# A router's tail and a fill: moving small steps between the queues of a two-router transformer block on one core

## Chip, cores and metric

One NeuronCore of a Trainium2 chip runs the whole program in one launch. The metric is the device time of one execution in microseconds. Engines: TensorE (PE; its weight loads are PEld), VectorE (DVE), ScalarE (ACT), GpSimd (POOL), and SyncE (SP), which only issues DMAs. ScalarE and GpSimd issue DMAs too, from their own instruction streams.

## What is computed

The input x is 4096 rows (8 x 512 tokens) of 256 floats. Three layers, each added to x; the first and the last share their weights:

```python
x = x + 0.5 * ffn(layernorm(x))       # first router and experts ("a")
x = x + attn_block(layernorm(x))      # the middle
x = x + 0.5 * ffn(layernorm(x))       # second router and experts ("b")

# ffn: 8 experts, capacity 256 rows each (0.5 * 4096 / 8)
probs  = softmax(x @ w_switch + b_switch); routes = argmax(probs)
pos    = running count of the rows of the same route, up to this row, minus 1
keep   = pos < capacity
out    = where(keep, relu(x @ w1[e] + b1[e]) @ w2[e] + b2[e], x)
out    = out * (pmax / stop_gradient(pmax))

# attn_block: linear attention over the 16 heads of a token (feature map elu + 1),
# output projection, residual, layernorm, gelu MLP of width 1024, residual
```

A row that no expert keeps is "passed": its result is x + 0.5 * layernorm(x) times a factor near one, an affine function of the row. The kernel computes it for every row and stores it to the output; the experts later overwrite the rows that they keep.

## The kernel before

Rows are taken in 32 tiles of 128 (token tiles 0 to 31), in 8 groups of four. The order of the program is fixed by hand, one instruction stream per engine, with semaphores between them.

**Stages.** The first router and its experts come first, up to about 170 us. The middle is a software pipeline of 43 steps (MID_STEPS, s = 0 to 42): in step s, tile s is loaded and its statistics taken, tile s-2 is turned and multiplied to queries, keys and values, tiles s-3 to s-5 go through the attention, s-6 is normalized for the MLP. The MLP of group g takes steps 10 + 4g to 13 + 4g, two of its eight hidden blocks a step; its last products are in step 41 with the second down product in step 42. Then the second expert phase runs to the end: SyncE reads back the routing table (L453), VectorE makes token numbers, GpSimd gathers rows (L625), they are normalized and turned, and TensorE runs eight experts without a pause.

**Exchange of queries, keys and values (the fill).** Attention mixes heads within a token, so the three matrices are written to DRAM by SyncE (`store_grids`, L495) and read back in another layout by many small DMAs. A tile needs one DMA for values, eight for keys (`issue_keys`, L335) and eight for queries (`issue_queries`, L341). For the first HELPED = 7 tiles ScalarE issues six of the eight queries of a tile, and for tile 0 also four of its keys (L978 to L988). For tile 0 it does so in step 3, which in its program order stands ahead of `turn_zn(2)` (L902 to L906) in step 4, the copy of the turned tile 2 to `xnts[0]`, the high half of its operand; VectorE makes the low half (L1395) and TensorE then multiplies (`qkv`, in step 4 ahead of `sum_kv(0)`). `sum_kv(n)` (L1733) waits for the keys and values of tile n, `sum_att(n)` for its queries.

**Gelus.** In each step 10 to 41 ScalarE runs two hidden blocks (`gelus`, L933: once as float to `hid`, L941, once rounded to `hids`, L944); GpSimd subtracts the two (`low_hidden`, L726); TensorE multiplies by the down weights. The exponential and the gelu lie in different tables of ScalarE, so each change from one to the other is an ACT_TABLE_LOAD.

**Second router.** For group g: statistics on VectorE (`stats`, L1022), the inverse roots on GpSimd (`roots_b`, L586, whose two operations are L591 and L593), logits by TensorE, the choice on VectorE (`choose`, L1034), the exponential on ScalarE (`soften`, L790), the count of earlier rows on TensorE, and the dispatch on VectorE (`dispatch`, L1073), which leaves in `entry_b` and `dest_b` what is to be written where in the routing table. GpSimd then writes it with one indirect DMA per tile (`send`, L608 to L615, to `table`), computes four factors (`pass_factors_b`, L595), and VectorE makes the passed rows in `pass_b` (`passed`, L1097), a buffer of four tiles whose places come free when an earlier store has landed; SyncE stores them in pairs (`store_passed`, L402). Groups 0 to 5 are passed within the steps: `passed_at(s)` names the two tiles whose sends and rows fall in step s, tiles 20 and 21 in step 40, 22 and 23 in step 41. The router of group 6 runs in steps 40 to 42 (its `soften` in step 41 between the two gelu pairs), that of group 7 behind the steps, and tiles 24 to 31 are sent and passed there.

**What closes the middle.** SyncE reads the table only when all sends (`s_bsent`), all passed rows' stores (`s_bstored`) and all stores of the residual rows x2 to `late_rows` (`s_x2s`) have landed; the other engines wait for the same semaphores.

Of the kernel before, what the change touches and what calls it, by code (L numbers as in the profile page):

```python
# [14 lines left out]
P = 128  # L15
# [12 lines left out]
def build(nc, x_in, ln1_w, ln1_b, wq, bq, wk, bk, wv, bv, wo, bo, ln2_w, ln2_b,  # L28
# [32 lines left out]
    with ExitStack() as ctx:  # L61
# [84 lines left out]
        s_bsent, s_bstored = sems("b_sent", 2), sems("b_stored", 2)  # L146
        one = {f: sem(f"experts_{f}") for f in ("table", "token", "stat", "root", "unit", "turned", "xt", "xtl",
# [180 lines left out]


# [60 lines left out]
        def _(sp):  # L390
# [11 lines left out]
            def store_passed(n):  # L402

                sp.wait_ge(s_bmade, n + 2)
                sp.dma_start(out_rows[n * P:(n + 2) * P, :].rearrange("(t p) d -> p t d", p=P),
                             pass_b[:, n % GROUP:n % GROUP + 2]).then_inc(s_bstored[n // 2 % 2], 16)

# [140 lines left out]
            for n in range(PASSED_IN_STEPS, NT, 2):  # L548
                store_passed(n)
# [3 lines left out]
            sp.wait_ge(s_bmade, NT)  # L553
# [13 lines left out]
        def _(pool):  # L567
# [166 lines left out]
            for s in range(MID_STEPS):  # L734
# [5 lines left out]
                for n in passed_at(s):  # L740
                    send(n)
# [11 lines left out]
                if group_at(s, 16) is not None:  # L753
                    roots_b(group_at(s, 16))
                if routed(s, 2) is not None:
                    pass_factors_b(routed(s, 2))


            roots_b(NG - 1)
            for n in range(PASSED_IN_STEPS, (NG - 1) * GROUP):  # L760
                send(n)
            pass_factors_b(NG - 1)
            for n in range((NG - 1) * GROUP, NT):
# [13 lines left out]
        def _(act):  # L777
# [148 lines left out]

            def copy_kvt(n):
# [22 lines left out]
            for s in range(MID_STEPS):  # L950
                if at(s, 2) is not None:
                    turn_zn(s - 2)
                g_up, j_up = divmod(s - 10, GROUP)
# [22 lines left out]
                if routed(s, 1) is not None:  # L976
                    soften(routed(s, 1))
                n = at(s, 3)  # L978
                if n is not None and n < HELPED:
                    act.wait_ge(s_grid[n % 2], 16 * (n // 2 + 1))  # L980
                    if n == 0:
                        act.wait_ge(s_zeros, 6)
                        for t in range(4, 8):
                            issue_keys(act, 0, t)
                    if n >= 2:
                        act.wait_ge(s_st2, n - 1)
                    for t in range(2, 8):
                        issue_queries(act, n, t)  # L988
# [12 lines left out]

            g = NG - 1
# [4 lines left out]
            identify(g)  # L1007

# [3 lines left out]
            act.wait_ge(s_bmade, NT)  # L1012
# [8 lines left out]
        def _(dve):  # L1021
# [51 lines left out]
            def dispatch(g):  # L1073
# [14 lines left out]
                if g >= 2:  # L1088
# [6 lines left out]
                                         op0=ALU.mult, op1=ALU.mult).then_inc(s_bdisp, 1)  # L1095

# [414 lines left out]
            for n in range(PASSED_IN_STEPS, NT):  # L1511
                passed(n)
# [435 lines left out]
```

## Time and profile before

| | |
|---|---|
| median of 3 runs | 772.32 us (770.03 to 772.68) |
| the profiled execution | 771.66 us |
| its span in the trace | 769.9 us |
| busy in the span | PE 87%, PEld 75%, DVE 58%, ACT 52%, POOL 42% |
| mean granted clock of TensorE | 0.94 of full |

All rows are of the one profiled execution, in microseconds from its span's start. The difference between its time and its span, 1.8 us, lies around the trace. A row of the timeline has the start, the length, the engine and line, the operation with its output and inputs, the count of merged instructions, and in brackets how long the engine stood idle before it and what ended that. A line number can be that of a small helper (L1527 is every matmul, L1539 every transpose), so tile names say which one it is. "q" behind an engine is its instruction queue, where DMA issues are.

### The profile page before, as it was taken

What the parts mean: (1) busy time and instruction counts of PE and PEld (TensorE: products, weight loads), DVE (VectorE), ACT (ScalarE), POOL (GpSimd) and SP (SyncE); (2) the same over time, 40 slices, a digit from 0 to 9 for tenths busy, and PEclk for the clock granted to TensorE, in tenths of its full rate; (3) what the DMA queues carried; (4) which work ended last, traced back from release to release, by engine and by line L of the source; (5) the groups of instructions that cost most, each with busy time, mean ns of one, the idle gap of its engine ahead of it and who ended that gap; (6) DMA issues with size and microseconds to landing.
All of it is one profiled execution on the core that took longest, in us unless ns stands there. A gap on an engine that the chain in (4) does not pass through costs nothing. (4 is left out here: it accounts for less than half of the span.)

```text
span 769.9 us, 17017 instructions
## 1 busy us (share of the span) xinstructions
PE 671.6 (87%) x6127; PEld 578.8 (75%) x6127; DVE 447.3 (58%) x1222; ACT 400.8 (52%) x805; POOL 326.5 (42%) x480
## 2 busy tenths in 40 slices
PE   7649999984777999999999999999999822999993
PEld 5437999973555888888888888888888712999993
DVE  7852756413477676767868677777565352444420
ACT  5753555512333667676766767666736510444430
POOL 6240573322132343444554745636456664133311
PEclk9759999996899999999999999999999975999997
DMA  8485677413665454544655455545415232466610
GB/s 261 141 277 174 199 253 237 135 38 75 100 110 92 80 83 84 93 82 65 108 79 126 66 110 91 97 78 95 81 42 169 91 117 42 132 205 198 209 59 28
DMA packets 284001, 92.43 MB, mean 120 GB/s; under 512 B 213933, under 2 KB 281636, under 8 KB 283918
## 3 DMA queue, kind: packets, MB, share of 16 engines
q1 hardware_dynamic: 267310, 82.26, 44.9%
q0 software_dynamic: 4096, 8.33, 3.4%
q10 hardware_dynamic: 12512, 0.76, 1.1%
q8 instruction: 50, 0.82, 0.4%
q14 instruction: 33, 0.27, 0.1%
HBM read 61.95 MB, written 29.41 MB: 119 GB/s over the span
## 5 line engine op out<-in xcount | busy, mean ns | idle before, releaser
L1527 PE MATMUL bank<-down_w,hids 128*128 128x256 f32 x768 | 107.9, 285 | 1.9 <-POOL hids L726 1.9
L726 POOL TENSOR_TENSOR hids<-hid,hids 128x512 fp32r<-128x512 f32 x64 | 83.1, 1298 | 54.2 <-ACT hids L944 54.0
L1527 PE MATMUL bank<-hnts,up_w 128*128 128x512 f32 x384 | 104.4, 407 | 0.0
L1527 PEld LDWEIGHTS bank<-down_w,hids 128*128 128x128 f32 x768 | 97.3, 188 | 5.5 <-POOL hids L726 3.5
L1527 PE MATMUL bank<-qkv_w,xnts 128*128 128x256 f32 (+1 forms) x384 | 80.9, 361 | 12.6 <-DVE xnts L1395 11.8
L1527 PEld LDWEIGHTS bank<-qkv_w,xnts 128*128 128x128 f32 x384 | 64.0, 199 | 25.6 <-DVE xnts L1395 14.0
L1527 PEld LDWEIGHTS bank<-hnts,up_w 128*128 128x128 f32 x384 | 67.6, 189 | 11.4
L941 ACT ACTIVATE hid<-bank,cols 128x512 f32<-128x512 f32 x64 | 44.1, 688 | 45.7 <-PE bank L1527 45.4
L717 POOL TENSOR_SCALAR sth<-sth 128x1 f32<-128x1 f32 x32 | 7.2, 225 | 129.9 <-DVE sth L1407 129.8
L1527 PE MATMUL bank<-b_w,xb_h 128*128 128x256 f32 x256 | 60.1, 379 | 0.0
L1527 PE MATMUL bank<-a_w,xa_h 128*128 128x256 f32 x256 | 60.1, 379 | 0.0
L1527 PE MATMUL bank<-xb_xt,b_w 128*128 128x256 f32 x384 | 58.0, 304 | 1.5 <-DVE xb_xt L1136 1.5
L1527 PE MATMUL bank<-xa_xt,a_w 128*128 128x256 f32 x384 | 58.1, 304 | 1.4 <-DVE xa_xt L1136 1.4
L825 ACT ACTIVATE xb_h<-bank,cols 128x256 f32<-128x256 f32 x64 | 26.9, 471 | 60.1 <-PE bank L1527 50.1
L1527 PEld LDWEIGHTS bank<-xa_xt,a_w 128*128 128x128 f32 x384 | 51.9, 199 | 3.7 <-DVE xa_xt L1136 1.8
L1527 PEld LDWEIGHTS bank<-xb_xt,b_w 128*128 128x128 f32 x384 | 51.9, 199 | 3.4 <-DVE xb_xt L1136 1.9
L825 ACT ACTIVATE xa_h<-bank,cols 128x256 f32<-128x256 f32 x64 | 26.8, 470 | 51.6 <-PE bank L1527 48.5
L1527 PEld LDWEIGHTS bank<-b_w,xb_h 128*128 128x128 f32 x256 | 46.3, 189 | 5.1
L1527 PEld LDWEIGHTS bank<-a_w,xa_h 128*128 128x128 f32 x256 | 46.3, 189 | 5.1
L906 ACT CAST xnts<-bank 128x256 fp32r<-128x256 f32 x32 | 12.0, 375 | 63.1 <-PE bank L1539 58.0
L1110 DVE TENSOR_TENSOR b_w<-b_raw,b_w 128x512 fp32r<-128x512 f32 x32 | 24.0, 751 | 35.8 <-ACT b_w L806 18.0
L944 ACT ACTIVATE hids<-bank,cols 128x512 fp32r<-128x512 f32 x64 | 43.6, 681 | 0.0
(246 smaller groups left out, 1426.2 us busy)
## 6 DMA issues: line engine op xcount, KB each, us to landing
qkv_rows<-feats SPq DMA_DIRECT2D x32, 384.0 KB, 3.5
a_raw<-in_L_ffn_w_dram SPq DMA_DIRECT2D x32, 256.0 KB
a_w<-in_L_ffn_w_dram SPq DMA_DIRECT2D x32, 256.0 KB
b_raw<-in_L_ffn_w_dram SPq DMA_DIRECT2D x32, 256.0 KB
b_w<-in_L_ffn_w_dram SPq DMA_DIRECT2D x32, 256.0 KB
mid_rows<-x_all SPq DMA_DIRECT2D x8, 512.0 KB
x<-mid_rows SPq DMA_DIRECT2D x32, 128.0 KB, 2.6
values<-qkv_rows SPq DMA_DIRECT2D x32, 128.0 KB
```

The costliest lines, as they stand in the source:

```text
L717: pool.tensor_scalar(st[:, 7:8], st[:, 7:8], EPS, None, ALU.add).then_inc(rs, 1)
L726: pool.tensor_tensor(hids[1][u % 3][:], hid[u % 2][:], f32(hids[0][u % 3][:]), ALU.subtract).then_inc(s_hidl, 1)
L825: act.activation(ex.buf.h[u % 4][:, i], dst[:, i * CAP:(i + 1) * CAP], ACT.Relu, bias=bias).then_inc(ex.sem.relu, 1)
L906: act.copy(xnts[0][n % 2][:], bank[B_TURN][:, 0:D].rearrange("p (k t) -> p k t", k=KD)).then_inc(s_xnh, 1)
L941: act.activation(hid[u % 2][:], bank[b][:], ACT.Gelu, bias=bias).then_inc(s_hid, 1)
L944: act.activation(hids[0][u % 3][:], bank[b][:], ACT.Gelu, bias=bias).then_inc(s_hid, 1)
L1110: dve.tensor_tensor(low[cut], ex.raw[cut], f32(high[cut]), ALU.subtract).then_inc(ex.sem.low1, 1)
L1527: return pe.matmul(dst, left, right, start=start, stop=stop, skip_group_check=True)
```

## The change

Three things move.

1. Fill: ScalarE's six query issues for tile 0 go from step 3 to step 4, behind `turn_zn(2)`. Its four key issues stay in step 3.
2. Second router, group 6: the exponential goes behind the gelus of step 41, the roots ahead of step 40's second subtraction, the count on TensorE behind the down product of step 41. GpSimd sends one tile in step 40 (20) and one in step 41 (21) instead of two; 22 to 25 follow behind the steps ahead of the roots of group 7, then 26 to 31.
3. Passed rows of groups 6 and 7: the factors are computed on VectorE behind the last dispatch, the rows of tiles 24 to 27 by ScalarE and of 28 to 31 by VectorE, and they overwrite their place in `x2` instead of going to `pass_b`. SyncE stores them from there.

```diff
@@ sync @@
+            def store_in_place(n):
+                g, first = n // GROUP, n % (2 * GROUP)
+                sp.wait_ge(s_bplace[g % 2], n % GROUP + 2)
+                sp.dma_start(out_rows[n * P:(n + 2) * P, :].rearrange("(t p) d -> p t d", p=P),
+                             x2[:, first:first + 2]).then_inc(s_bstored[n // 2 % 2], 16)
             for n in range(PASSED_IN_STEPS, NT, 2):
-                store_passed(n)
+                store_in_place(n)
...
-            sp.wait_ge(s_bmade, NT)
+            sp.wait_ge(s_bmade, PASSED_IN_STEPS)
@@ gpsimd, LAST_SENT = PASSED_IN_STEPS - GROUP @@
-                for n in passed_at(s):
-                    send(n)
+                if group_at(s, 16) == NG - 2:
+                    roots_b(NG - 2)
+                if s < MID_STEPS - 3:
+                    for n in passed_at(s):
+                        send(n)
+                if s == MID_STEPS - 2:
+                    send(LAST_SENT + 1)
...
                     low_hidden(g_up, 2 * j_up + 1)
-                if group_at(s, 16) is not None:
+                if s == MID_STEPS - 3:
+                    send(LAST_SENT)
+                if group_at(s, 16) is not None and group_at(s, 16) < NG - 2:
                     roots_b(group_at(s, 16))
-                if routed(s, 2) is not None:
+                if routed(s, 2) is not None and routed(s, 2) < NG - 2:
                     pass_factors_b(routed(s, 2))
+            for n in range(LAST_SENT + 2, PASSED_IN_STEPS + 2):
+                send(n)
             roots_b(NG - 1)
-            for n in range(PASSED_IN_STEPS, (NG - 1) * GROUP):
-                send(n)
-            pass_factors_b(NG - 1)
-            for n in range((NG - 1) * GROUP, NT):
+            for n in range(PASSED_IN_STEPS + 2, NT):
                 send(n)
@@ scalar @@
+            def help_queries(n):
+                act.wait_ge(s_grid[n % 2], 16 * (n // 2 + 1))
+                if n >= 2:
+                    act.wait_ge(s_st2, n - 1)
+                for t in range(2, 8):
+                    issue_queries(act, n, t)
             for s in range(MID_STEPS):
                 if at(s, 2) is not None:
                     turn_zn(s - 2)
+                if s == 4:
+                    help_queries(0)
...
-                if routed(s, 1) is not None:
+                if routed(s, 1) is not None and routed(s, 1) < NG - 2:
                     soften(routed(s, 1))
...
+                if s == 3:
+                    act.wait_ge(s_grid[0], 16)
+                    act.wait_ge(s_zeros, 6)
+                    for t in range(4, 8):
+                        issue_keys(act, 0, t)
+                if at(s, 3) is not None and 1 <= s - 3 < HELPED:
+                    help_queries(s - 3)
...
+            soften(NG - 2)
             g = NG - 1
...
             soften(g)
             identify(g)
+            for n in range(PASSED_IN_STEPS, (NG - 1) * GROUP):
+                g, i = divmod(n, GROUP)
+                act.wait_ge(s_bfac, 4 * (g + 1))
+                act.wait_ge(s_x2s[g % 2], 16 * (g // 2 + 1))
+                row = x2[:, n % (2 * GROUP)]
+                act.activation(row, row, ACT.Identity, bias=fac_b[g % 2][:, 2, i:i + 1],
+                               scale=fac_b[g % 2][:, 3, i:i + 1]).then_inc(s_bplace[g % 2], 1)
@@ vector: pass_factors_b as on GpSimd before, and @@
+            def passed_in_place(n):
+                g, i = divmod(n, GROUP)
+                dve.wait_ge(s_bfac, 4 * (g + 1))
+                dve.wait_ge(s_bturn, n + 1)
+                dve.wait_ge(s_x2s[g % 2], 16 * (g // 2 + 1))
+                row = x2[:, n % (2 * GROUP)]
+                dve.tensor_scalar(row, row, fac_b[g % 2][:, 3, i:i + 1], fac_b[g % 2][:, 2, i:i + 1], ALU.mult,
+                                  ALU.add).then_inc(s_bplace[g % 2], 1)
             dispatch(g)
-            for n in range(PASSED_IN_STEPS, NT):
-                passed(n)
+            pass_factors_b(NG - 2)
+            pass_factors_b(NG - 1)
+            for n in range((NG - 1) * GROUP, NT):
+                passed_in_place(n)
@@ tensor @@
                 g = routed(s, 1)
-                if g is not None:
+                if g is not None and g < NG - 2:
                     pe.wait_ge(*kv_free)
                     count(g, bank[B_KV])
...
                     down_mid(g_up, 2 * j_up)
+                if g == NG - 2:
+                    pe.wait_ge(*kv_free)
+                    count(g, bank[B_KV])
+                    kv_free = (s_bdisp, 9 * g + 1)
```

## Rows read from the trace of the kernel before

**Rows 1.** Chain that ended last, in order of time: start, length, what.
```profile
634.13 2.13 DMA table<-rb_entry,rb_dest
636.31 2.74 DMA xb_table<-table
...
650.14 6.99 PE bank L1527 x36
```

**Rows 2.** Timeline, steps 41 and 42.
```profile
611.31 1.55 PE L1527 MATMUL bank<-hnts,up_w 128*128 128x512 f32 x6
...
611.60 0.19 DVE L1039 TENSOR_TENSOR rb_lg<-bank,rb_rstd 128x32 f32<-128x32 f32 x1 [1.32 <-POOL rb_rstd L593]
...
613.55 1.28 ACT L941 ACT_TABLE_LOAD   x1
...
614.84 0.69 ACT L941 ACTIVATE hid<-bank,cols 128x512 f32<-128x512 f32 x1
...
616.00 0.62 ACT L806 CAST b_w<-b_raw 128x512 fp32r<-128x512 f32 x1
616.19 1.26 POOL L726 TENSOR_TENSOR hids<-hid,hids 128x512 fp32r<-128x512 f32 x1 [0.76 <-ACT hids L944]
...
617.50 1.71 PE L1527 MATMUL bank<-down_w,hids 128*128 128x256 f32 x12 [1.62 <-POOL hids L726]
617.92 0.18 DVE L1071 TENSOR_TENSOR rb_cnt<-bank,rb_hot 128x32 f32<-128x32 f32 x1
...
619.25 1.42 DVE L1419 TENSOR_TENSOR x_<-bank,xr 128x256 f32<-128x256 f32 x4
```

**Rows 3.** Timeline, behind the steps, to the last send.
```profile
622.34 0.23 POOL L591 TENSOR_SCALAR rb_rstd<-rb_mv 128x4 f32<-128x4 f32 x1 [2.40 <-DVE rb_mv L1032]
...
623.80 0.19 DVE L1039 TENSOR_TENSOR rb_lg<-bank,rb_rstd 128x32 f32<-128x32 f32 x1 [1.54 <-POOL rb_rstd L593]
...
626.54 0.20 DVE L1094 SCALAR_TENSOR_TENSOR rb_entry<-rb_small 128x4 f32<-128x4 f32 x1
...
629.94 1.46 DVE L1103 TENSOR_SCALAR rb_pass<-x_,rb_fac 128x256 f32<-128x256 f32 x4 [1.66 <-DMA out_dram<-rb_pass]
630.16 1.10 POOL L613 DMA_INDIRECT table<-rb_entry,rb_dest  x1 [0.34 <-issue]
...
634.13 0.97 POOL L613 DMA_INDIRECT table<-rb_entry,rb_dest  x1 [0.30 <-issue]
```

**Rows 4.** Timeline, fill, ScalarE's queue, ScalarE and TensorE.
```profile
189.49 3.17 ACTq L341 DMA_DIRECT2D queries<-qkv_rows  x6
...
193.03 0.37 ACT L906 CAST xnts<-bank 128x256 fp32r<-128x256 f32 x1 [5.11 <-issue]
...
193.92 4.21 PE L1527 MATMUL bank<-qkv_w,xnts 128*128 128x512 f32 x12 [5.97 <-DVE xnts L1395]
```

**Rows 5.** Timeline of SyncE's queue, keys of tiles 1 and 6.
```profile
194.69 4.50 SPq L335 DMA_DIRECT2D keys<-qkv_rows  x8
...
241.44 5.86 SPq L335 DMA_DIRECT2D keys<-qkv_rows  x8
```

**Rows 6.** Waits of SyncE's queue, 186 to 300: total, times, longest.
```profile
SPq L505 <- DMA qkv_rows<-feats: 14.9, 8, 3.5
...
SPq L495 <- DVE feats L1465: 1.0, 3, 0.4
```

**Rows 7.** Timeline of TensorE's weight loads, `sum_kv(6)`.
```profile
250.18 0.81 PEld L1527 LDWEIGHTS bank<-keys,values 128*32 128x32 f32 x32 [0.52 <-DMA keys<-qkv_rows]
```

**Rows 8.** Line L863: ns min/median/max; tile rb_pass from 626 to 632: landing.
```profile
L863 ACT ACTIVATE x_all<-x_all,ra_small x32: 583/586/604, 27.6 to 46.0; 128x256 f32<-128x256 f32 x32
...
DMA to landing us min/median/max: 2.2/2.2/2.2
```

**Rows 9.** Windows, 629.5 to 630: busy per engine, clock, DMA share, GB/s.
```profile
629.50:630.00 0.50, 0.00 (x0) 0.00 (x0) 0.06 (x1) 0.00 (x0) 0.33 (x2) 0.50 1.01 340
```

**Rows 10.** Windows, 650 to 658, same columns.
```profile
652.00:654.00 2.00, 2.00 (x12) 2.00 (x11) 0.74 (x2) 0.89 (x3) 0.10 (x1) 0.50 0.00 0
654.00:656.00 2.00, 2.00 (x12) 2.00 (x12) 0.69 (x1) 0.79 (x2) 0.00 (x0) 0.56 0.00 0
656.00:658.00 2.00, 2.00 (x18) 1.97 (x18) 0.69 (x1) 1.85 (x6) 0.00 (x0) 1.00 0.41 131
```

More of the change, by code:

```diff
@@ L146, in build @@
         s_bsent, s_bstored = sems("b_sent", 2), sems("b_stored", 2)
+        s_bplace = sems("b_passed_in_place", 2)
         one = {f: sem(f"experts_{f}") for f in ("table", "token", "stat", "root", "unit", "turned", "xt", "xtl",
@@ L327, in build @@
         PASSED_IN_STEPS = (NG - 2) * GROUP
+        LAST_SENT = PASSED_IN_STEPS - GROUP
         HELPED = 7
@@ L975, in _ @@
                     copy_kvt(0)
-                if routed(s, 1) is not None:
+                if routed(s, 1) is not None and routed(s, 1) < NG - 2:
                     soften(routed(s, 1))
[L978 to L988, printed above, removed]
+                if s == 3:
[5 more added lines that the diff above has]
+                    help_queries(s - 3)
                 for n in turned_at(s, 0):
@@ L1007, in _ @@
             identify(g)
+            for n in range(PASSED_IN_STEPS, (NG - 1) * GROUP):
[5 more added lines that the diff above has]
+                               scale=fac_b[g % 2][:, 3, i:i + 1]).then_inc(s_bplace[g % 2], 1)
             for i in range(2):
                 act.wait_ge(s_bsent[i], 64 * (NG // 2))
-            act.wait_ge(s_bmade, NT)
+            act.wait_ge(s_bmade, PASSED_IN_STEPS)
             for i in range(2):
@@ L1095, in dispatch, with pass_factors_b @@
                                          op0=ALU.mult, op1=ALU.mult).then_inc(s_bdisp, 1)
+            def pass_factors_b(g):
+                w, wm, shift, factor = (fac_b[g % 2][:, i] for i in range(4))
+                dve.wait_ge(s_bdisp, 9 * (g + 1))
+                dve.wait_ge(s_bfac, 4 * g)
+                dve.tensor_tensor(w, entry_b[g % 2][:, :, 1], rstd_b[g % 2][:], ALU.mult).then_inc(s_bfac, 1)
+                dve.wait_ge(s_bfac, 4 * g + 1)
+                dve.tensor_tensor(wm, w, mv_b[g % 2][:, :, 0], ALU.mult).then_inc(s_bfac, 1)
+                dve.tensor_scalar(factor, w, 1.0, None, ALU.add).then_inc(s_bfac, 1)
+                dve.wait_ge(s_bfac, 4 * g + 2)
+                dve.tensor_scalar(shift, wm, -1.0, None, ALU.mult).then_inc(s_bfac, 1)
+            def passed_in_place(n):
[6 more added lines that the diff above has]
+                                  ALU.add).then_inc(s_bplace[g % 2], 1)
             def passed(n):
```

## The prediction

> **What bounds the kernel now.** I read the chain that ended last first. Behind the middle of the kernel it is one straight line: the last send of routing entries lands at 634.13 + 2.13 = 636.26 us, the table is read back at 636.31, rows are gathered and normalized, and from 650.14 on TensorE multiplies to the end [rows 1]. So every microsecond by which the table read comes earlier is a microsecond of the span, if nothing behind it changes, and nothing behind it is edited. The timeline then shows what holds the table read. In step 41, the last with up-projections, ScalarE swaps to its exponential table and back for one small activation: TensorE's product is ready at 611.31 + 1.55 = 612.86, the load back ends at 614.83 and the gelu starts at 614.84 [rows 2]. The exponential was late because VectorE's choice waited 1.32 us for the inverse roots of GpSimd, which stood behind two sends and a subtraction [rows 2]. TensorE stood 1.62 us before its last down product at 617.50 [rows 2]. After that comes the router of the last group, entries at 626.74, and then GpSimd alone: sends of 0.97 us with 0.30 us between them, 1.28 us from start to start, the last at 634.13 [rows 3]. In the fill I read ScalarE's queue beside TensorE: six query issues take 3.17 us from 189.49, the high half of token tile 2 (the third xnts) follows at 193.03, and TensorE has stood 5.97 us when its product starts at 193.92 [rows 4].
>
> **Fill: the six issues go behind the third high half.** Nothing is added or removed: ScalarE starts the cast at about 189.5 instead of 193.03, 3.5 us earlier, and TensorE its product at 190.4. SyncE's queue is passed by none of this, and that is why I take zero. From 194.69 SyncE sends rows, stores and eight key loads per tile back to back: eight keys cost between 4.50 and 5.86 us [rows 5]. Of its waits between 186 and 300 us, 14.9 us are for the landing of its own stores and only 1.0 for VectorE's features [rows 6], so compute hardly paces it. The keys of tile 6, issued from 241.44 to 247.30, are what TensorE's weight load at 250.18 waits for (0.52 us, ended by the keys) [rows 5, 7]. A TensorE that runs 3.5 us ahead at 190 meets the same keys by then. Bounds: 3.5 us of gain if the keys were no limit, and a loss if ScalarE's issues for tile 1, now some 3.5 us earlier and so inside SyncE's window from 194.69, slow SyncE: at most 5.86 - 4.50 = 1.36 us for a tile [rows 5]. I take 0, nearest to the row at 250.18.
>
> **Steps 40 and 41.** GpSimd takes the roots of group 6 ahead of the second subtraction and only one send a step instead of two. The roots move ahead of that subtraction, so VectorE's choice, at 611.60 before, loses its wait of 1.32 us for them [rows 2]. ScalarE runs the last gelu right behind TensorE's product: 612.9 instead of 614.84, 1.9 us earlier. GpSimd's subtraction followed the gelu by 616.19 - 614.84 = 1.35 us, TensorE the subtraction by 1.31 us [rows 2]: 614.3 and 615.6. The single send between two subtractions (1.28 us after 612.6) ends at 613.8 and fits. TensorE fills 612.9 to 614.9 with the count and the other down product, which cost 0.4 and 1.7 us. The exponential itself pays a table load of 1.28 us behind the gelus (over at 614.2) and the weight cast of 0.62 us [rows 2]: it is over at 616.3. From the reading of the counts to the residual sum VectorE took 619.25 - 617.92 = 1.33 us [rows 2]; a first part of that lies before the exponential, so dispatch and count update are over at 617.5. The residual sum, 619.25 before, needs TensorE (615.6 + 1.7 = 617.3) and VectorE (617.5) [rows 2]. **Term: 1.75 us gained.** Both engines arrive within 0.2 us of each other, so nothing is to spare. Group 7's exponential then finds its table loaded; its load before was hidden behind the roots, so that counts nothing.
>
> A weighing of a rule: the row shows the load at 613.55 lasting 1.28 us and the gelu 0.01 us behind it, so a swap costs 1.28 us here [rows 2]. The Trainium skill (ScalarE: Activation LUTs, What ACT_TABLE_LOAD costs) adds a drain of 1.38 us to every switch, 2.66 in all. By that the exponential behind the gelus would be over 1.4 us later and the sum would be 3.1 us of gain instead of 4.5; this trace disagrees with the drain.
>
> **GpSimd behind step 41.** Four sends (22 to 25) start at 615.7 and end with 4 x 1.28 at 620.8. The statistics of group 7 were ready for the roots at 622.34 [rows 3]; 1.75 earlier is 620.6. So the roots start at 620.9, **0.3 us given back**, 1.45 gained. Roots to choice took 623.80 - 622.34 = 1.46, choice to entry 626.74 - 623.80 = 2.94 [rows 3]: choice at 622.35, entries at 625.3. Sends 26 and 27 lie between (622.5 to 625.0) and hide; before, all four sends of group 6 and the pass factors stood there and held send 28 until 630.16, 3.4 us behind the entries [rows 3]. Now send 28 starts at 625.4 and send 31 at 625.4 + 3 x 1.28 = 629.25 against 634.13: **4.9 us gained**, the 1.45 in it. The landing took 2.13 us with an empty queue [rows 1]. Now it shares the queues with the last stores of passed rows; its bounds are 0 and another 1 us (a store takes 2.2 us from issue to landing, and a send that meets one could see up to half of it [rows 8]). I take 0.4 us: last landing 631.8, **table read 4.5 us earlier**.
>
> **Factors and rows in place.** VectorE gets eight small operations behind the entries; by the spacing of the small ones in the router, about 0.12 us each, factors of group 6 at 625.8 and 7 at 626.3. Two places make the rows: ScalarE four of group 6, costed by the rows of the first stage, 0.586 us each [rows 8], done by 628.2; VectorE four of group 7, 1.46 us for four [rows 3], done by 627.8. Neither waits for a buffer; before, four rows waited 1.66 us for a store [rows 3]. What they wait for instead is that the store of x2 has landed, and that one is issued right behind the residual sum, over 6 us before. SyncE issues four stores at 627.0, 627.8, 628.3 and 628.8; landing 2.2 us later [rows 8] is 631.0. By volume, 1 MB at 340 GB/s [rows 9] is 3.1 us from about 628.2: 631.3. So this path lies 0.1 to 0.5 us below the sends: hidden, with a thin cover. If it were 1 us late, it would set the table read and cost 0.5 us. The final wait of SyncE and ScalarE on passed rows is shortened to 24 tiles and costs nothing.
>
> **Sum.** 0 (fill) - 4.5 (end of the middle) = -4.5 us against the profiled execution: 771.66 (span 769.9, 1.8 around it) becomes 767.2. The median of the runs is 772.32, 0.66 above that execution, so 767.8. Bounds of the main case: 5.0 gained with a landing of 2.13, 3.5 with a landing 1.4 us longer. TensorE's granted clock adds a scatter that no edit sets: after the long wait it stood at half level (1.2 GHz) and rose between 654 and 656, some 5 us after the products began at 650.14 [rows 1, 10]. A rise two microseconds sooner or later would move the end by one, since half the rate does half the work; the three runs spread over 2.65 us.
>
> **The rivals.**
> (a) The fill pays: the keys would come in time after all. For it: TensorE's 5.97 us stand is real [rows 4], and the first product there also starts closer to the one before, so it may find the higher clock. Against: the wait for keys at 250.18 [rows 7]. With 2.5 of the 3.5 us kept, 765.3.
> (b) The end gives only part: the sends' landing, the rows in place on ScalarE, or the exponential take the place of the removed waits. Place: the table read. If the passed rows or the exponential chain come 2 us later than worked out, the gain is 2.5 and the time 769.8. For it: three chains meet within 0.5 us of each other. In its own sentence, one form of it: VectorE's rows in place while GpSimd makes descriptors. The rows show sends of 0.97 us alone and 1.10 beside VectorE's rows at 629.94 [rows 3], 0.1 us; if instead the four rows (1.46 us) held the sends up wholly, the gain would be 3.0 and the time 769.3, 3 in 100. The Trainium skill (SBUF — State Buffer, SBUF: two separate sides) has that rule: GpSimd cannot write descriptors while VectorE holds the shared port with such an operation. The rows here bear out a tenth of it.
> (c) Slower: ScalarE's query issues fall into SyncE's key issues and slow them. Place: the fill, keys of tiles 1 to 7. Price: 1.36 us a tile [rows 5], 7 x 1.36 = 9.5 us, less 4.5: 5.0 slower, 777.3. It turns the sign from the fourth tile on (4.5 / 1.36 = 3.3). Against: only the first one or two tiles are shifted, since TensorE's lead is gone at the next keys.
> (d) The edits do not reach the chain, because another wait (store of x2, storing of passed rows) holds the table read: 772.3.
>
> **How the numbers follow.** Main case 0.62, (a) 0.08, (b) 0.22, (c) 0.05, (d) 0.03. A measurement of this kernel can tell about 0.5%, 3.9 us. The main case at 4.5 with half a microsecond of doubt passes that in nine tenths: 0.56 + 0.08 from (a) = 0.64 faster; (c) gives 0.05 slower; the rest, 0.31, is within. The range reaches from 765.5 (5.0 gained, and the scatter of the clock, or (a)) to 770.3 (case (b)), and leaves out (c), (d) and the far end of (a).
>
> **What would show it.** Right: in the fill TensorE's product of tile 2 starts near 190.4, yet the keys' product of tile 6 stays near 250.2, with a wait ended by keys. The last gelu 0.1 us behind its product; no table load between the gelus of step 41; residual sum near 617.5; roots of group 7 right behind send 25 at 620.9; last send near 629.3; no stand of VectorE before its last rows; table read near 631.8. Wrong: a table read held by the stores of passed rows, keys earlier or later than 250 by over 1 us, or roots of group 7 after 622.

## The result, and the profile after

The changed kernel takes 765.15 us (median of 5 runs, 763.97 to 766.51), the kernel before 770.29 us in the same rounds (median of 5, 769.61 to 772.68). The ratio is 0.9925, interval 0.9902 to 0.9949: 5.1 us faster by the medians, 5.8 by the ratio. A second series of the change has 0.9935 (0.9922 to 0.9948), 5.0 us. The forecast was 767.8 us with a range of 765.5 to 770.3: the way was right and the gain of 4.5 us close to what was measured, but the time lies 0.35 us under the range. The kernel before was no longer at 772.32: with two more runs its median is 770.29, and four later series of it have 769.51 to 770.90.

The profiled execution of the changed kernel took 766.51 us, span 764.8. First the end of the middle, in the order of the prediction. The timeline of the changed kernel around steps 41 and 42 (lines are of the changed program: L1578 is every matmul, L735 GpSimd's subtraction, L622 its send):

```profile
605.45 1.05 POOL L602 TENSOR_TENSOR rb_rstd<-rb_rstd,minus_half 128x4 f32<-128x4 f32 x1
...
609.11 0.18 DVE L1067 TENSOR_TENSOR rb_lg<-bank,rb_rstd 128x32 f32<-128x32 f32 x1
...
610.22 1.56 PE L1578 MATMUL bank<-hnts,up_w 128*128 128x512 f32 x6
610.29 1.28 POOL L735 TENSOR_TENSOR hids<-hid,hids 128x512 fp32r<-128x512 f32 x1 [0.17 <-ACT hids L966]
...
610.44 1.18 DVE L1082 TENSOR_TENSOR rb_hot<-first_wins,rb_best 128x32 bf16<-128x32 f32 x1
...
611.82 0.69 ACT L963 ACTIVATE hid<-bank,cols 128x512 f32<-128x512 f32 x1 [1.53 <-PE bank L1578]
...
613.61 1.28 ACT L809 ACT_TABLE_LOAD   x1
...
614.48 1.69 PE L1578 MATMUL bank<-down_w,hids 128*128 128x256 f32 x12 [1.03 <-POOL hids L735]
...
616.49 1.42 DVE L1468 TENSOR_TENSOR x_<-bank,xr 128x256 f32<-128x256 f32 x4
```

Against [rows 2]: the roots are done at 606.50, so VectorE's choice at 609.11 has no wait for them; the last gelu starts at 611.82, 0.04 us behind the product that ends at 611.78; the table load stands behind the gelus at 613.61. TensorE still stands ahead of its last down product, but 1.03 us instead of 1.62. The residual sum follows the first gelu of step 41 (608.93) by 7.56 us; before, that gelu started at 609.80 and the distance was 619.25 - 609.80 = 9.45. Behind the steps:

```profile
618.69 0.97 POOL L622 DMA_INDIRECT table<-rb_entry,rb_dest  x1 [0.30 <-issue]
...
619.69 0.24 POOL L600 TENSOR_SCALAR rb_rstd<-rb_mv 128x4 f32<-128x4 f32 x1
...
621.16 0.19 DVE L1067 TENSOR_TENSOR rb_lg<-bank,rb_rstd 128x32 f32<-128x32 f32 x1 [1.66 <-POOL rb_rstd L602]
...
623.88 0.16 DVE L1122 SCALAR_TENSOR_TENSOR rb_entry<-rb_small 128x4 f32<-128x4 f32 x1
...
624.56 2.08 ACT L1034 ACTIVATE x_<-x_,rb_fac 128x256 f32<-128x256 f32 x4 [2.18 <-DVE rb_fac L1135]
...
624.88 0.98 POOL L622 DMA_INDIRECT table<-rb_entry,rb_dest  x1 [1.27 <-DVE rb_entry L1122]
...
625.23 1.38 DVE L1143 TENSOR_SCALAR x_<-x_,rb_fac 128x256 f32<-128x256 f32 x4
625.68 2.41 SPq L414 DMA_DIRECT2D out_dram<-x_  x4
626.16 0.97 POOL L622 DMA_INDIRECT table<-rb_entry,rb_dest  x1 [0.31 <-issue]
...
628.72 0.97 POOL L622 DMA_INDIRECT table<-rb_entry,rb_dest  x1 [0.30 <-issue]
630.99 0.37 SPq L462 DMA_DIRECT2D xb_table<-table  x1
```

Against [rows 3]: the roots of group 7 start 0.03 us behind send 25, which is the send at 618.69; VectorE and ScalarE make their rows with no wait for a buffer; the last send is at 628.72 and the table is read at 630.99, 22.06 us behind the first gelu of step 41 instead of 26.51. That is 4.45 us, against 4.5 forecast for this part. What SyncE waited for last, by its own waits in the stretch (total, times, longest), is the stores first and then, for 0.3 us, the sends:

```profile
SPq L564 <- DMA out_dram<-x_: 2.4, 1, 2.4
SPq L566 <- DMA table<-rb_entry,rb_dest: 0.3, 1, 0.3
```

The fill is the second half. The same stretch as [rows 4], and on to the keys of tiles 1 and 3:

```profile
187.33 0.37 ACT L921 CAST xnts<-bank 128x256 fp32r<-128x256 f32 x1 [2.42 <-issue]
187.36 3.03 ACTq L344 DMA_DIRECT2D queries<-qkv_rows  x6
...
188.22 4.21 PE L1578 MATMUL bank<-qkv_w,xnts 128*128 128x512 f32 x12 [3.94 <-DVE xnts L1444]
...
199.98 1.82 PE L1578 MATMUL bank<-keys,values 128*32 128x128 f32 x32 [2.50 <-DMA keys<-qkv_rows]
...
202.08 3.04 PE L1578 MATMUL bank<-qkv_w,xnts 128*128 128x512 f32 x12
...
219.78 1.17 PE L1578 MATMUL bank<-keys,values 128*32 128x128 f32 x32 [1.60 <-DMA keys<-qkv_rows]
...
221.22 3.66 PE L1578 MATMUL bank<-qkv_w,xnts 128*128 128x512 f32 x12
```

The cast now stands ahead of the six issues, and TensorE's product of tile 2 starts after a stand of 3.94 us instead of 5.97. But TensorE then stands 2.50 us for the keys of tile 1 and 1.60 us for those of tile 3, where it had stood 0.56 us and less before. And its clock falls behind these stands: the product of tile 3 at 202.08 took 3.04 us and that of tile 5 at 221.22 took 3.66 us, where others take 2.37.

### The profile page after: what moved, and what is told of

The parts are those of the page before. It is cut to its first block, busy times and chain, and to the rows that moved or that the text cites. A ratio compares the mean times of both kernels' runs of the same rounds, so it can differ in the third digit from the quotient of the medians.

```text
span 764.8 us, 17021 instructions
## 1 busy us (share of the span) xinstructions
PE 672.3 (88%) x6127; PEld 580.9 (76%) x6127; DVE 446.1 (58%) x1226; ACT 400.6 (52%) x807; POOL 325.4 (43%) x472
## 4 chain that ended last, share of the span: by engine, by line
PE 56%; issue 5%; DMA 4%; POOL 3%; DVE 3%; ACT 3%; SPq 2%; ACTq 1%; POOLq 0%; DVEq 0%
PE bank L1578 51%; PE bank L1590 5%; DMA qkv_rows<-feats 2%; SPq L338 2%; POOL hids L735 1%; ACTq L344 1%; POOL table L622 1%; DMA keys<-qkv_rows 1%; DMA xb_rows<-late_rows,xb_token 0%; ACT hids L966 0%; ACT feats L936 0%; DMA xb_table<-table 0%; ACT ots L989 0%; DMA mid_rows<-xa_fin,xa_slot 0%; DMA table<-rb_entry,rb_dest 0%
## 5 line engine op out<-in xcount | busy, mean ns | idle before, releaser
L1578 PE MATMUL bank<-down_w,hids 128*128 128x256 f32 x768 | 107.8, 285 | 1.3 <-POOL hids L735 1.3
L735 POOL TENSOR_TENSOR hids<-hid,hids 128x512 fp32r<-128x512 f32 x64 | 83.1, 1299 | 54.7 <-ACT hids L966 54.5
L1578 PE MATMUL bank<-hnts,up_w 128*128 128x512 f32 x384 | 104.5, 407 | 0.0
L1578 PEld LDWEIGHTS bank<-down_w,hids 128*128 128x128 f32 x768 | 97.3, 188 | 4.9 <-POOL hids L735 2.9
L1578 PE MATMUL bank<-qkv_w,xnts 128*128 128x256 f32 (+1 forms) x384 | 81.9, 364 | 9.2 <-DVE xnts L1444 8.4
L1578 PEld LDWEIGHTS bank<-qkv_w,xnts 128*128 128x128 f32 x384 | 64.9, 202 | 21.9 <-DVE xnts L1444 10.0
L1578 PEld LDWEIGHTS bank<-hnts,up_w 128*128 128x128 f32 x384 | 67.6, 189 | 11.4
L1578 PE MATMUL bank<-b_w,xb_h 128*128 128x256 f32 x256 | 60.1, 379 | 0.0
L1578 PE MATMUL bank<-a_w,xa_h 128*128 128x256 f32 x256 | 60.1, 379 | 0.0
L1578 PE MATMUL bank<-xb_xt,b_w 128*128 128x256 f32 x384 | 58.2, 304 | 1.5 <-DVE xb_xt L1185 1.5
L1578 PE MATMUL bank<-xa_xt,a_w 128*128 128x256 f32 x384 | 57.7, 303 | 1.4 <-DVE xa_xt L1185 1.4
L1578 PEld LDWEIGHTS bank<-xb_xt,b_w 128*128 128x128 f32 x384 | 52.0, 199 | 3.4 <-DVE xb_xt L1185 1.9
L1578 PEld LDWEIGHTS bank<-xa_xt,a_w 128*128 128x128 f32 x384 | 51.6, 198 | 3.7 <-DVE xa_xt L1185 1.8
L1578 PEld LDWEIGHTS bank<-b_w,xb_h 128*128 128x128 f32 x256 | 46.3, 189 | 5.1
L1578 PEld LDWEIGHTS bank<-a_w,xa_h 128*128 128x128 f32 x256 | 46.3, 189 | 5.1
L1514 DVE SCALAR_TENSOR_TENSOR feats<-bank,feats 128x512 f32<-128x512 f32 x32 | 22.1, 691 | 37.9 <-ACT feats L938 37.9
```

Source lines behind the costliest of these rows:

```text
L735: pool.tensor_tensor(hids[1][u % 3][:], hid[u % 2][:], f32(hids[0][u % 3][:]), ALU.subtract).then_inc(s_hidl, 1)
L1514: dve.scalar_tensor_tensor(out=soft, in0=bank[B_QK][:], scalar=0.0, in1=soft, op0=ALU.max, op1=ALU.add).then_inc(s_feat, 1)
L1578: return pe.matmul(dst, left, right, start=start, stop=stop, skip_group_check=True)
```

## Experiments

All of them are built on one of the two kernels; "ratio" is to the kernel before in the same rounds. Since the edits are local, each profile is also cut at fixed events, in us: A, the first load of a row of the middle (all before it is untouched everywhere); B, from SyncE's first key load of tile 0 to the first gelu of step 41 (the fill and the steps); C, from there to the table read; D, from the first product of the second expert phase to the end of the span (untouched everywhere). Between A and B lie another 16.1 to 17.2 us that no edit touches, and between C and D 13.7 to 14.0.

| kernel | A | B | C | D |
|---|---|---|---|---|
| before, shown ahead | 171.37 | 422.33 | 26.51 | 119.76 |
| before again | 169.26 | 422.80 | 26.55 | 119.97 |
| change | 169.08 | 423.43 | 22.06 | 119.94 |
| change again | 169.63 | 421.69 | 22.32 | 119.03 |
| fill only | 169.25 | 423.91 | 27.18 | 118.99 |
| fill only again | 169.38 | 421.72 | 26.59 | 118.58 |
| end only | 169.41 | 422.15 | 22.06 | 118.84 |
| change, fill delayed | 169.74 | 420.40 | 22.06 | 119.72 |
| the same again | 169.56 | 420.93 | 22.08 | 119.45 |
| change, store first | 169.87 | 421.29 | 22.66 | 118.97 |
| change, delay and store first | 169.37 | 423.02 | 22.02 | 118.65 |
| change, rows not in place | 168.70 | 422.98 | 24.03 | 118.58 |
| change, exponential between | 168.69 | 424.39 | 24.32 | 119.93 |
| change, sends paired | 169.97 | 421.68 | 23.87 | 119.59 |

### Halves of the change

Fill only, on the kernel before:

```diff
+                if s == 4:
+                    help_queries(0)
...
-                if n is not None and n < HELPED:
+                if at(s, 3) is not None and 1 <= s - 3 < HELPED:
```

> Only the fill edit, on the kernel before. Theory A (SyncE's queue paces the fill): TensorE's product of tile 2 starts about 3.5 us sooner behind the keys of tile 0, but sum_kv of tile 6 comes within 1 us of where it was behind the keys of tile 0 (62.7 us behind, 250.18 - 187.47), and the time stays within 1 us of before: ratio 0.9990 to 1.0010. Rival B (the fill pays): up to 3.5 us less, ratio down to 0.9955, sum_kv(6) 2.5 us or more sooner. Rival C (ScalarE's earlier issues or stores landing behind queries slow SyncE): 1 to 4 us more, ratio 1.0013 to 1.005.

769.19 us (median of 11) against 769.51, ratio 0.9984 (0.9969 to 1.0): 0.3 us less by the medians and 1.2 by the ratio, while its profile has B at 423.91, over 1 us longer than before. So a second time:

> The fill edit alone, again, for a second profile and more rounds. Theory A: within 1.2 us of before (ratio 0.9985 to 1.0015); TensorE stands 2 us or more ahead of the keys' product of tile 1 and its clock falls there. Rival B (the fill edit is worth the 1 us that the first rounds hinted at, 0.9984 with an interval of 0.9969 to 1.0): ratio 0.9985 or less again.

769.09 us (median of 12) against 770.77, ratio 0.9978 (0.9966 to 0.999), and B at 421.72. By the two ratios the fill edit is worth 1.2 and 1.7 us, against my zero, and B lies 2 us apart in two profiles of one program. The kernel before against itself shows how far such a ratio strays:

> The kernel before as it is, against itself: ratio 0.999 to 1.001, which shows how far such a ratio strays. Theory A (the first profile of before was a slow draw in the untouched first stage, 171.4 us to the first row load where eleven profiles of other kernels have 168.7 to 170.0): 168.7 to 170.0 now, profiled time 769 to 770.5. Rival B (before has a slower first stage than every edited kernel): 171 again. Keys of tile 0 to first gelu of step 41 near 422.2, no half-clock stretch behind 208 us in either case.

770.85 against 770.9, ratio 0.9993 (0.9978 to 1.0008), A at 169.26, B at 422.80. So the first profile of the kernel before had a long A by 2 us. The time of this one, 771.34, lies above what was expected all the same: its span is 768.6, and 2.7 us lie around it instead of 1.8. The fill edit's 1.2 and 1.7 us stand against a stray of 0.5 us; only the second series excludes zero.

End only, which is the change without the lines above:

> The change without its fill edit. Theory A: the whole gain is here, ratio 0.993 to 0.9945 (4.3 to 5.3 us less); from the first gelu of step 41 to the table read 22.1 us, as in the changed kernel (630.99 - 608.93), against 26.5 before (636.31 - 609.80). Rival B: 2.5 us of the gain is the fill's, ratio 0.9965 or more. Rival C: more gain than the change has, ratio under 0.992.

765.31 us (median of 7) against 769.51, ratio 0.995 (0.9932 to 0.9967), C at 22.06. The ratio lies just over the 0.9945 that was expected, with an interval that holds it. The stretch C gives 4.45 us on the trace and the time gave 3.9 us by the ratio: the end carries the bulk of the gain, and 1 us or so is left for the fill.

The change again, beside the next three:

> The changed kernel as it is, again, beside the three others on the same chip: ratio to before 0.991 to 0.995. The two theories of the fill tell apart by its second profile only: from the keys of tile 0 to the first gelu of step 41 the first one showed 423.4 us against 422.3 before. If the fill edit costs, it is over 423 again; if that was scatter, it lies anywhere from 420.5 to 424.

765.53 us against 770.82, ratio 0.9935, B at 421.69, 1.74 us less than in the first profile. So the long B of that one is not a fixed cost of the edit.

### What the fill is paced by

Delayed: 14 activations of one column ahead of the third high half put TensorE's stand back.

```diff
             for s in range(MID_STEPS):
+                if s == 4:
+                    for i in range(14):
+                        if i >= 1:
+                            act.wait_ge(s_idle, i)
+                        act.activation(idle[:], minus_half[:, 0:1], ACT.Exp).then_inc(s_idle, 1)
```

> The change with 14 tiny activations of ScalarE ahead of the third high half, about 3.6 us (0.2 us each and a hand-over), which puts TensorE's stand of the kernel before back without moving the query issues. Theory A (a TensorE that is early in the fill meets the same keys): same time as the change, ratio to before 0.992 to 0.9945, sum_kv(6) at the same distance from the keys of tile 0. Rival B (the stand costs what it lasts): 2.5 to 3.6 us more than the change, ratio 0.996 to 0.9975. Rival C (an early TensorE does harm through ScalarE's issues): faster than the change by 1 us or more, ratio 0.991 or less.

> The change with the 14 tiny activations, as before, for a second profile and more rounds. Theory A (TensorE's early product is not worth anything): ratio within 0.0015 of the change's 0.9925 and 0.9935, no half-clock stretch behind the keys of tile 1, keys of tile 0 to first gelu of step 41 420 to 421.5. Rival B (the first profile was a lucky one): 422 or more.

764.45 us, ratio 0.9926 (0.9906 to 0.9947), and 764.63 us, ratio 0.9916 (0.9899 to 0.9933). TensorE's product of tile 2 starts 3.1 us later than in the change, and that costs nothing that can be measured; B is 420.40 and 420.93, under both profiles of the change. Its timeline of TensorE:

```profile
192.71 4.21 PE L1585 MATMUL bank<-qkv_w,xnts 128*128 128x512 f32 x12 [7.65 <-DVE xnts L1451]
196.85 1.56 PE L1585 MATMUL bank<-keys,values 128*32 128x128 f32 x32
...
202.57 1.08 PE L1585 MATMUL bank<-keys,values 128*32 128x128 f32 x32 [0.56 <-DVE att_ L1438]
...
204.37 2.38 PE L1585 MATMUL bank<-qkv_w,xnts 128*128 128x512 f32 x12 [0.34 <-DVE xnts L1451]
```

TensorE stands 7.65 us in one piece, then the keys of tile 1 are there (0.56 us, for VectorE), and the next product runs at full clock in 2.38 us. In the change the same time is stood in two pieces, and the second piece comes with half clock.

The edit does one thing more than was expected of it. The query issues of tile 0 stand behind the same activations, so they move too: they start 4.91 us behind SyncE's first keys, against 1.8 to 2.1 us in every other kernel of the table below, with the fill edit or without. SyncE's keys of tile 1 come sooner in the two delayed profiles (6.71 and 6.74 us behind those of tile 0, against 7.2 to 7.6 in the others). So the delay could have cost something that the later queries gave back; no run parts the two. What becomes of TensorE's lead is seen without the delay, in us behind SyncE's first keys:

| kernel | product of tile 2 | keys' product, tile 1 | tile 2 | tile 6 |
|---|---|---|---|---|
| before | 6.45 | 15.96 | 24.10 | 62.71 |
| before again | 6.06 | 16.16 | 24.32 | 62.95 |
| end only | 6.07 | 15.79 | 23.93 | 62.59 |
| change | 2.72 | 14.48 | 23.59 | 63.77 |
| change again | 2.71 | 14.56 | 23.61 | 61.86 |
| fill only | 2.72 | 14.66 | 23.70 | 64.27 |
| fill only again | 2.90 | 14.36 | 23.46 | 61.97 |
| change, fill delayed | 5.80 | 15.66 | 23.80 | 61.93 |
| the same again | 5.80 | 15.80 | 23.93 | 62.12 |

A lead of about 3.4 us is 1.5 at the keys of tile 1 and 0.5 at those of tile 2: the keys take it away, as forecast.

Store first: SyncE's loop shortened by taking the row load out of it.

```diff
-                if at(s, -2) is not None:
+                if at(s, -2) is not None and not 3 <= s < 12:
                     load_row(s + 2)
                 if at(s, 2) is not None:
                     store_grids(s - 2)
+                if 3 <= s < 12:
+                    load_row(s + 2)
```

> The change, and in steps 3 to 11 SyncE stores a tile's queries, keys and values ahead of loading the row of the later tile, so that the load (0.45 us and a gap of 0.1) lies in the wait for the store's landing. Theory A (SyncE's loop of store, landing, values and eight keys paces the fill): 0.5 us less for each of 7 tiles until compute paces it: 1 to 3 us less than the change, ratio to before 0.989 to 0.9915. Rival B (the fill is paced by compute, or the stores' landing only moves): within 0.5 us of the change.

764.26 us (762.51 to 769.05), ratio 0.9924 (0.9901 to 0.9946), against 0.9935 of the change beside it: 0.85 us by the ratios, 1.27 by the medians, and the intervals overlap, so the two are not apart. SyncE did run ahead: its store of tile 4 lies 28.8 us behind the keys of tile 0 instead of 30.6 in the change's profile beside it. But the keys' product of tile 6 came at 61.5 instead of 61.9, and between 186 and 262 us SyncE now waited 3.9 us for ScalarE's and VectorE's features, where it had waited 0.4. With SyncE faster, compute paces the fill: the two chains are nearly equal.

> The change with both the 14 tiny activations ahead of the third high half and SyncE's store ahead of the row load in steps 3 to 11. Theory A (early TensorE only stands later, for the keys of tile 1, and falls to half clock there; SyncE's loop is the other pace): the fill is the shortest of all: keys of tile 0 to first gelu of step 41 420 us or less (423.4 and 421.7 in two profiles of the change, 420.4 with the delay alone, 421.3 with the store first alone), ratio to before 0.9885 to 0.992. Rival B (scatter only): 421 to 424 and the ratio of the change, 0.9925 to 0.9935.

765.45 us, ratio 0.9938 (0.992 to 0.9955), B at 423.02. A miss: the two do not add. Its clock fell for a second stretch between 216 and 236 us, as in the three other profiles with B at 423.4 and over. Windows of that stretch (busy time of each engine, then the granted clock, the DMA share and GB/s), of the change, the change again, this kernel, the exponential between, and fill only:

```profile
216.00:236.00 20.00, 14.95 (x186) 11.82 (x186) 13.01 (x34) 6.50 (x16) 5.42 (x12) 0.91 0.59 95
```
```profile
216.00:236.00 20.00, 15.61 (x222) 12.28 (x225) 14.80 (x38) 6.41 (x16) 5.43 (x12) 1.00 0.61 98
```
```profile
216.00:236.00 20.00, 15.27 (x186) 11.66 (x186) 12.69 (x35) 6.33 (x16) 5.41 (x12) 0.91 0.55 92
```
```profile
216.00:236.00 20.00, 15.56 (x179) 12.33 (x180) 12.22 (x33) 6.60 (x16) 5.42 (x12) 0.83 0.54 91
```
```profile
216.00:236.00 20.00, 14.84 (x185) 11.54 (x183) 12.58 (x34) 6.35 (x16) 5.41 (x12) 0.91 0.58 95
```

All profiles with the clock at 1.00 there have B between 420.4 and 422.98, the four with 0.83 to 0.91 have 423.02 to 424.39. So the second stretch at half clock goes with the upper end of the scatter; the 2.6 us among the others it does not explain. Nor does the clock fall by itself. Just ahead of the fall TensorE had stood in one piece, 1.60 and 1.92 us for the keys of tile 3 in the change and in fill only, 1.70 and 1.82 us for the rows of the MLP (`hnts`) in the other two; the ten others stood there 1.61 us at most. In the change and in fill only these keys were late because SyncE issued them 5.2 and 5.9 us behind the store of their tile, where the change again has 3.7.

### What the end is made of

The changed kernel with each part undone.

Rows not in place (all eight on VectorE into the four-place buffer, ScalarE's four taken out, factors still on VectorE):

```diff
-                store_in_place(n)
+                store_passed(n)
...
-            for n in range((NG - 1) * GROUP, NT):
-                passed_in_place(n)
+            for n in range(PASSED_IN_STEPS, NT):
+                passed(n)
```

> The change with the eight passed rows of groups 6 and 7 back in the four-place buffer and all on VectorE (factors stay on VectorE). Theory A (in place takes away the wait for a buffer): rows 24 to 27 done at 626.3 as counted in the changed kernel, the next four wait for two landings to about 628.3, last store issued at 630, landed near 632.3: table read 23.4 to 24.0 us behind the first gelu of step 41 instead of 22.06, so 1.3 to 1.9 us more than the change; ratio to before near 0.9945 to 0.9955. Rival B (the sends alone hold the table read): 22.1, the same time as the change.

767.09 us, ratio 0.996 (0.9946 to 0.9973). C is 24.03, 1.97 more than the change's:

```profile
628.65 1.59 DVE L1144 TENSOR_SCALAR rb_pass<-x_,rb_fac 128x256 f32<-128x256 f32 x4 [2.29 <-DMA out_dram<-rb_pass]
...
632.70 0.37 SPq L462 DMA_DIRECT2D xb_table<-table  x1
```
```profile
SPq L564 <- DMA out_dram<-rb_pass: 1.8, 1, 1.8
```

The last send is where it was (628.47, 19.80 us behind the first gelu of step 41 as against 19.79), the second four rows wait 2.29 us for a landing, and SyncE's last wait is for the stores. So in place is worth 2 us beside the earlier sends. In the kernel before, SyncE waited 1.1 us more for the sends after its stores had landed, so alone it should gain nothing there; that was not run.

Exponential between the gelu pairs:

```diff
-                if routed(s, 1) is not None and routed(s, 1) < NG - 2:
+                if routed(s, 1) is not None:
                     soften(routed(s, 1))
...
-            soften(NG - 2)
```

> The change with the exponential of group 6 back between the gelu pairs of step 41. Theory A: the two table loads and the exponential (1.28 + 0.23 + 1.28) stand behind the first pair, whose end is 1.2 us behind its start; the second pair starts about 4.2 us behind the first instead of 2.9, residual sum 1.3 us later, table read 1.2 to 1.4 us later (23.3 to 23.5 behind the first gelu of step 41): 1.3 us more than the change. Rival B (the page's drain at every switch): 2.7 us or more later. Rival C (GpSimd's sends in a row hold the roots of group 7 anyway): under 0.5 us later.

768.26 us (765.19 to 770.37), ratio 0.9965 (0.9951 to 0.9979). C is 24.32, 2.26 more, where 1.3 was expected:

```profile
609.70 0.69 ACT L963 ACTIVATE hid<-bank,cols 128x512 f32<-128x512 f32 x1 [1.16 <-PE bank L1577]
...
611.07 1.28 ACT L809 ACT_TABLE_LOAD   x1
...
612.36 0.23 ACT L809 ACTIVATE rb_ex<-rb_sub 128x32 f32<-128x32 f32 x1
...
612.61 1.28 ACT L963 ACT_TABLE_LOAD   x1
...
613.90 0.69 ACT L963 ACTIVATE hid<-bank,cols 128x512 f32<-128x512 f32 x1
...
616.57 2.93 PE L1577 MATMUL bank<-down_w,hids 128*128 128x256 f32 x12 [2.35 <-POOL hids L735]
```

The second pair starts 4.2 us behind the first, as expected, and TensorE's stand is 2.35 us instead of 1.03. The last down product then took 2.93 us instead of 1.69: its clock had fallen. The wait brings 1.32 us and the clock 1.24; 0.3 of the sum was covered, since in the change the residual sum stood behind VectorE's own work and not behind this product. The expected 1.3 us had the wait and not the clock. Load and activation follow each other within 0.02 us on both sides of the exponential.

Sends paired (two a step in steps 40 and 41, two ahead of the roots of group 7):

```diff
-                if s < MID_STEPS - 3:
-                    for n in passed_at(s):
-                        send(n)
-                if s == MID_STEPS - 2:
-                    send(LAST_SENT + 1)
+                for n in passed_at(s):
+                    send(n)
...
-                if s == MID_STEPS - 3:
-                    send(LAST_SENT)
...
-            for n in range(LAST_SENT + 2, PASSED_IN_STEPS + 2):
+            for n in range(PASSED_IN_STEPS, PASSED_IN_STEPS + 2):
```

> The change with two sends a step again in steps 40 and 41 (two instead of four ahead of the roots of group 7). Theory A (GpSimd's subtraction is behind the sends on the path to TensorE): in step 40 the subtraction starts at about 609.3 instead of 607.35 by the changed kernel's times, and in step 41 1.1 us or more behind where it was; residual sum 8.7 us or more behind the first gelu of step 41 instead of 7.56, table read 1 to 3 us later than the change's 22.1 to 22.3; ratio 0.9945 to 0.997. If TensorE's longer stand makes its clock fall it is the upper end. Rival B (the four sends ahead of the roots of group 7 cost what they save): within 0.3 us of the change.

767.81 us, ratio 0.9962 (0.9947 to 0.9977), C at 23.87, 1.81 more:

```profile
607.47 1.38 POOL L622 DMA_INDIRECT table<-rb_entry,rb_dest  x1 [0.30 <-issue]
...
608.58 2.86 DVE L1070 TENSOR_TENSOR rb_sub<-rb_lg,rb_best 128x32 f32<-128x32 f32 x1
608.88 2.51 POOL L735 TENSOR_TENSOR hids<-hid,hids 128x512 fp32r<-128x512 f32 x2
...
610.21 1.70 PE L1573 MATMUL bank<-down_w,hids 128*128 128x256 f32 x12 [1.87 <-POOL hids L735]
```

The second subtraction of step 40 starts at 608.88, behind both sends and 0.50 us behind the first gelu of step 41 (608.38); in the change it started 1.58 us ahead of it. TensorE stands 1.87 us for it, where in the change only its weight load stood, for 0.24 us. Undone one at a time, the three parts cost 1.97, 2.26 and 1.81 us of C, 6.0 together, of a gain of 4.45, so their worths do not add. Part of the excess shows: 1.24 us are the clock's. And each of these kernels has an order that the kernel before did not have. Before, with the sends paired too but the roots behind the subtraction, it started at 608.41, 1.39 us ahead of its gelu:

```profile
608.41 1.31 POOL L726 TENSOR_TENSOR hids<-hid,hids 128x512 fp32r<-128x512 f32 x1
```

## Why the prediction was right or wrong, point by point

**The sum's base: the step that failed, and it put the time out of the range.** I took the median of three runs, 772.32, as the level and added 0.66 us to the profiled execution. The level measured 770.29 with two more runs, 2.0 us lower, and a second profile has the untouched first stage at 169.26 instead of 171.37. The difference, -4.5, was nearly right; measured are -5.1 by the medians and -5.8 by the ratio. From 770.29 it gives 765.8, 0.6 us from the result. The lower bound, 765.5, was 2.3 us under the forecast. The 5.0 us of gain and the 1 us for the clock that I named make 766.3; the rest leaned on rival (a), and nothing was set aside for a wrong level, though the five runs of the kernel before lie 3 us apart.

**Fill at zero: probably a term mis-sized by about 1 us; where it comes from stays open.** That an early TensorE meets keys that come no sooner stood up: its lead of 3.4 us is 0.5 us at the keys of tile 2. The keys' product of tile 6, which was to stay, came 63.8 and 61.9 us behind the keys of tile 0 in two profiles of the change, 62.7 and 63.0 before; the first is 1.06 us later, just over my own sign of being wrong, the other 0.85 sooner. Two series of the fill edit alone gave 0.9984 and 0.9978. Profiles of it without a second half-clock stretch have B at 421.7, 0.6 to 1.1 us under before; those with one are 0.6 to 1.6 us over. But the untouched 16 to 17 us ahead of B scatter by 1.1 us as well, and counted from A the change again is where the first profile of before is, 438.43 us. The runs, not the profiles, carry this gain. Later query issues of tile 0 do not explain it: these start 1.86 and 1.85 us behind the keys in the change, 2.02 and 1.76 before. Rival (a) had the way right with half the size, and its reason is not shown. Rival (c) did not show: SyncE's eight keys took 4.53 and 4.71 us with ScalarE's issues beside them.

**Steps 40 and 41: right.** Forecast 1.75 us, measured 9.45 - 7.56 = 1.89. The gelu behind its product, the single send that fits, the table load behind the gelus, all as worked out.

**Sends ahead of the roots of group 7: right, smaller.** 0.3 us given back were forecast; statistics were ready at 619.50, the roots started at 619.69.

**Behind the entries: right in sum, two errors against each other.** Entries lay 15.1 us behind the first gelu of step 41 against 15.5 forecast. Send 28 did not start 0.1 us behind them but 0.84 us. So the last send is 19.79 us behind the gelu against 19.45. The landing took 2.22 us against 2.55, and the table read came at 22.06 against 22.0.

**Rows in place: right.** Their cover was forecast at 0.1 to 0.5 us; SyncE waited 0.3 us for the sends after the stores had landed. That it is thin is also right: take in-place away and the stores set the end. Rivals (b) and (d), an end of the middle that gives only part or nothing, did not come: C lost 4.45 us.

**The weighings.** The switch between the exponential and the gelu cost 1.28 us, the length of its load, wherever it stood: in the change at 613.61 with the exponential at 614.90, and twice in the kernel with the exponential between. The drain that the Trainium skill (ScalarE: Activation LUTs, What ACT_TABLE_LOAD costs) adds to each switch shows in none of the profiles.

In the change, sends 28 and 29 beside VectorE's rows take 0.98 and 0.97 us, as sends 30 and 31 do alone. The 1.10 us that I put down to VectorE's rows is what a send costs behind another kind of instruction: 1.04 us at 606.07 in the kernel before, with nothing of VectorE beside it, and 1.04 to 1.11 throughout that profile. Longer are only the two sends of the change that start inside a two-input operation of VectorE of 1.3 us, 1.32 us at 608.81 and 1.25 at 614.59. So the 1.5 us of my rival's price were not paid. By the Trainium skill (SBUF — State Buffer, SBUF: two separate sides) GpSimd cannot write descriptors while VectorE holds the port that the two share. Beside VectorE's rows that cost nothing here; whether they held that port, no row says.

Between two computing operations there is such a hold. VectorE's two-input operation at 610.44 took 1.18 us instead of 0.19 and ended with GpSimd's subtraction at 611.6; with the sends paired, one took 2.86 us beside two subtractions. By the Trainium skill (SBUF — State Buffer, SBUF: two separate sides) a VectorE operation with two inputs in SBUF and a GpSimd operation that reads SBUF exclude each other. The traces agree.

## What to carry to other kernels

Before a stand of one engine is costed, find out whether the next thing it meets is paced by another queue: the same idle time then mostly moves, here from 190 to 200 us. And take the level of a forecast from as many runs as there are and from the scatter they show; a single profile can be 2 us high in a stage that the change never touches. Where three chains meet within half a microsecond, undoing any one of them can cost alone about half of what all three gave, so their worths must not be added. And an experiment that delays one instruction delays all that stand behind it in its queue: look in the trace what else has moved.

## What was not expected of the hardware

A stand of TensorE costs more than its length when its clock falls with it. Ahead of a down product stands of 1.62 and 1.87 us left it at full level (1.71 and 1.70 us for twelve products), one of 2.35 us was followed by a product of 2.93 us, most of it at half level; in the fill stands of 2.50 and 1.60 us were followed by products of 3.04 and 3.66 us. Whether it falls differs between executions of one program: 0.91 and 1.00 mean granted clock in 216 to 236 us in two of the change, and 1.7 us in B between them. D, a stretch that no edit touches, lies between 118.58 and 119.97 us over the fourteen profiles.

A send that has to wait for VectorE's entry starts 0.84 us behind it (624.04 to 624.88), while one that stands ready follows its forerunner in 0.30 us. The same hand-over stands ahead of the first gather behind the table read: the token numbers end at 634.01, the gather starts at 634.82.
